# A graph layer fed by GpSimd gathers: whole-table VectorE passes move to ScalarE, and the gather ring grows from 26 to 27 quads

## What is computed

```python
h = jnp.maximum(_layernorm(x), 0.0)                      # x: 12500 nodes x 128
C = 0.5 * (jnp.cos(edge_weight * PI / CUTOFF) + 1.0)     # 212500 edges
W = (ssp(edge_attr @ mlp_w1 + mlp_b1) @ mlp_w2 + mlp_b2) * C[:, None]
xp = h @ lin1_w
agg = segment_sum(xp[src] * W, dst, num_segments=12500)  # dst is sorted
out = x + (ssp(agg @ lin2_w + lin2_b) @ lin_w + lin_b)   # ssp(v) = softplus(v) - log 2
```

## Time and profile before

| | us |
|---|---|
| median of 3 runs | 2056.18 |
| lowest and highest run | 2053.5, 2058.3 |
| the profiled execution, device time | 2054.31 |
| its span, first to last instruction | 2052.4 |
| GpSimd busy | 1539.9 |
| TensorE, VectorE, ScalarE busy | 1302.4, 1081.9, 910.0 |

### The profile page before, as it was taken

The page is one execution under the profiler, slowest core; times in us unless marked ns, Lnnn a source line. Parts: engine busy times, 40 slices in busy tenths (PEclk is TensorE's granted clock), DMA queues, the critical chain, the costliest instruction groups (busy, mean ns, idle before and its releaser), DMA issues.

```text
span 2052.4 us, 51157 instructions
## 1 busy us (share of the span) xinstructions
PE 1302.4 (63%) x12671; PEld 1108.5 (54%) x12879; DVE 1081.9 (53%) x3364; ACT 910.0 (44%) x1536; POOL 1539.9 (75%) x1629
## 2 busy tenths in 40 slices
PE   6567666766676666656666666666656556666565
PEld 5455555555555555545555555555545445555454
DVE  8766655555555555545544445545444445454444
ACT  6664444444444444444443444434443444343442
POOL 7777777777777777777777777777777777777775
PEclk9887988888888788777887877887888788787887
DMA  9632333333333333333333333333332332333321
GB/s 319 233 88 77 85 89 78 85 90 80 90 89 79 84 88 80 91 90 80 82 90 79 90 89 79 86 85 80 89 90 71 89 89 72 89 79 82 88 72 47
DMA packets 118412, 190.46 MB, mean 93 GB/s; under 512 B 34784, under 2 KB 66000, under 8 KB 117988
## 3 DMA queue, kind: packets, MB, share of 16 engines
q0 software_dynamic: 51968, 106.53, 21.0%
q1 hardware_dynamic: 63076, 79.85, 13.2%
q10 hardware_dynamic: 3072, 0.79, 0.2%
HBM read 174.24 MB, written 12.80 MB: 91 GB/s over the span
## 4 chain that ended last, share of the span: by engine, by line
POOL 37%; issue 19%; PE 11%; SPq 10%; ACT 8%; DVE 7%; ACTq 4%; DVEq 2%; DMA 1%; POOLq 0%
POOL XG L435 37%; SPq L393 7%; ACTq L508 4%; PE PA L801 3%; PE PW L787 3%; PE PX L770 3%; SPq L389 2%; ACT TB L523 2%; ACT TB L521 2%; DVE XG L684 2%; ACT TB L519 2%; DVEq L656 1%; PE PW L784 1%; ACT XG L457 1%; DVE TB L575 1%
## 5 line engine op out<-in xcount | busy, mean ns | idle before, releaser
L435 POOL DMA_INDIRECT XG<-xp_scratch,IX x1560 | 1476.0, 946 | 475.8 <-issue 469.7
L684 DVE SCALAR_TENSOR_TENSOR XG<-PW,CC,XG 128x128 f32<-128x128 f32 x1624 | 456.8, 342 | 442.4 <-DMA XG<-xp_scratch,IX 425.7
L519 ACT ACTIVATE TB<-PX 128x512 f32<-128x512 f32 x416 | 245.7, 591 | 968.8 <-PE PX L770 477.6
L787 PE MATMUL PW<-W,TB 128*128 128x128 f32 x3322 | 538.8, 315 | 106.5 <-DVE XG L684 79.4
L787 PEld LDWEIGHTS PW<-W,TB 128*128 128x128 f32 x3322 | 535.2, 230 | 18.1
L784 PE MATMUL PW<-BPB,ones 128*128 128x512 bf16 (+1 forms) x209 | 98.9, 473 | 566.3 <-DVE XG L684 548.9
L784 PEld LDWEIGHTS PW<-BPB,ones 128*128 128x128 bf16 x416 | 40.7, 98 | 744.2 <-issue 737.1
L652 DVE SCALAR_TENSOR_TENSOR TB<-PX,TB 128x512 f32<-128x512 f32 x416 | 283.9, 682 | 274.6 <-ACT TB L523 266.8
L801 PE MATMUL PA<-OH,XG 128*64 128x64 f32 x6480 | 317.7, 271 | 0.0
L523 ACT ACTIVATE TB<-TB,HALF 128x512 f32<-128x512 f32 x416 | 299.7, 720 | 13.5
L801 PEld LDWEIGHTS PA<-OH,XG 128*64 128x64 f32 x6480 | 286.8, 182 | 32.3 <-issue 21.1
(11 more groups left out here) (86 smaller groups left out, 495.2 us busy)
## 6 DMA issues: line engine op xcount, KB each, us to landing
HT<-xp_scratch SPq DMA_DIRECT2D x3092, 0.5 KB
AT<-attr_t SPq DMA_DIRECT2D x206, 200.0 KB
XG<-xp_scratch,IX POOLq DMA_INDIRECT x1560
HA<-xp_scratch ACTq DMA_DIRECT2D x1536, 0.5 KB
AG<-zero SPq DMA_DIRECT2D x1, 6400.0 KB, 22.8
xp_scratch<-XG SPq DMA_DIRECT2D x24, 256.0 KB, 2.9
XR<-x SPq DMA_DIRECT2D x24, 256.0 KB, 5.0
out<-XR SPq DMA_DIRECT2D x24, 256.0 KB, 2.6
```

What stands on the lines that cost most here:

```text
L435: e.indirect_dma_start(XG[q % XG_N][0:p, k * D:(k + 1) * D], None, xp, bass.IndirectOffsetOnAxis(ap=IX[0:p, t0 + k:t0 + k + 1], axis=0)).t ...
L519: e.activation(T[:, 0:w], PX[q % X1_N][:, 0:w], ACT.Abs).then_inc(s_ab, 1)
L684: ins = e.scalar_tensor_tensor(out=G, in0=PW[q % 2][0:p, k * D:(k + 1) * D], scalar=CC[0:p, t0 + k:t0 + k + 1], in1=G, op0=ALU.mult, op1=A ...
L787: ins = e.matmul(P[0:p, k * D:(k + 1) * D], TB[q % TB_N][:, k * TILE:k * TILE + p], W2[:, :], start=False, stop=(k == n - 1), skip_group_c ...
```

## The change

- **Ring:** XG_N goes from 26 to 27 quads.
- **Turns:** the two rounding passes leave VectorE and are two Copy activations on ScalarE (`turns`), ahead of its chunk 22. VectorE's last pass stays, and is cut into four pieces of some 416 columns. VectorE waits for `s_ck`.
- **Places:** the casts of the base and destination tables leave VectorE for ScalarE (`places`), ahead of its chunk 32. The base is also cast into a PSUM bank (`BQ`), and the subtraction that forms REL reads the base from there and not from SBUF.
- **Flags:** the test for places outside the window leaves VectorE. ScalarE takes Abs(REL - 31.5) and Relu(2|.| - 63) at step 18 (`far`), which writes VB directly. The product of flags and cutoff moves into the repair path.
- **First layer:** for quads 0 and 1 TensorE waits for the last rectifier only, not for ScalarE's last copies.

```diff
-    XG_N, TB_N, X1_N, OH_N = 26, 4, 4, 2
+    XG_N, TB_N, X1_N, OH_N = 27, 4, 4, 2
...
+        MID = sb("MID", [128, 2])
+        BQ = PF[:, 0:NQ]
...
+            def turns():
+
+                e.wait_ge(s_tb, 16)
+                e.activation(CK[:, :], CC[:, :], ACT.Copy, scale=0.05, bias=MAGIC).then_inc(s_ck, 1)
+                e.wait_ge(s_ck, 1)
+                e.activation(CK[:, :], CK[:, :], ACT.Copy, bias=-MAGIC).then_inc(s_ck, 1)
+
+            def places():
+
+                e.wait_ge(s_dx, 16 * (11 + 2 * AT_N))
+                e.activation(BF[:, :], BI[:, :], ACT.Copy).then_inc(s_di, 1)
+                e.activation(BQ, BI[:, :], ACT.Copy).then_inc(s_di, 1)
+                e.activation(REL[:, :], DI[:, :], ACT.Copy).then_inc(s_di, 1)
+
+            def far():
+
+                e.wait_ge(s_rel, 2)
+                for p, a, b in ((TILE, 0, NT - 1), (EDGES - (NT - 1) * TILE, NT - 1, NT)):
+                    e.activation(CK[0:p, a:b], REL[0:p, a:b], ACT.Abs, bias=MID[0:p, 0:1]).then_inc(s_far, 1)
+                e.wait_ge(s_far, 2)
+                for p, a, b in ((TILE, 0, NT - 1), (EDGES - (NT - 1) * TILE, NT - 1, NT)):
+                    e.activation(VB[0:p, a:b], CK[0:p, a:b], ACT.Relu, scale=2.0, bias=MID[0:p, 1:2]).then_inc(s_vb, 1)
...
-                e.wait_ge(s_cst, 1)
-                e.wait_ge(s_cw, 1)
+                e.wait_ge(s_cw, 4)
...
             for c in range(NPC + 3):
+                if c == NNC - 3:
+                    turns()
                 if c == NNC + 5:
                     cutoff()
+                if c == NNC + 7:
+                    places()
...
+                if i == FLAG_STEP:
+                    far()
...
             norms(0, NNC)
             e.wait_ge(s_tb, 16)
-            link(e.tensor_scalar(CK[:, :], CC[:, :], 0.05, MAGIC, ALU.mult, ALU.add))
-            link(e.tensor_scalar_add(CK[:, :], CK[:, :], -MAGIC))
-            e.scalar_tensor_tensor(out=CK[:, :], in0=CC[:, :], scalar=0.05, in1=CK[:, :],
-                                   op0=ALU.mult, op1=ALU.subtract).then_inc(s_cw, 1)
+            e.wait_ge(s_ck, 2)
+            for a in range(0, NT, -(-NT // 4)):
+                b = min(NT, a - (-NT // 4))
+                e.scalar_tensor_tensor(out=CK[:, a:b], in0=CC[:, a:b], scalar=0.05, in1=CK[:, a:b],
+                                       op0=ALU.mult, op1=ALU.subtract).then_inc(s_cw, 1)
...
-            e.tensor_copy(BF[:, :], BI[:, :])
-            link(e.tensor_copy(REL[:, :], DI[:, :]))
+            e.memset(VB[:, NT - 1:NT], 0.0).then_inc(s_rel, 1)
+            e.wait_ge(s_di, 3)
             nf = NT // QT
-            rel = REL[:, 0:nf * QT].rearrange("p (q t) -> p q t", t=QT)
-            link(e.tensor_tensor(rel, rel, BF[:, 0:nf].unsqueeze(2).to_broadcast([128, nf, QT]), ALU.subtract))
             if NT % QT:
                 link(e.tensor_scalar(REL[:, nf * QT:NT], REL[:, nf * QT:NT], BF[:, nf:nf + 1], None, ALU.subtract))
+            rel = REL[:, 0:nf * QT].rearrange("p (q t) -> p q t", t=QT)
+            e.tensor_tensor(rel, rel, BQ[:, 0:nf].unsqueeze(2).to_broadcast([128, nf, QT]), ALU.subtract).then_inc(s_rel, 1)
...
-                if i == FLAG_STEP:
-
-                    link(e.memset(CK[:, NT - 1:NT], 0.0))
-                    for p, a, b in ((TILE, 0, NT - 1), (tail, NT - 1, NT)):
-                        link(e.tensor_scalar(CK[0:p, a:b], REL[0:p, a:b], WIN - 0.5, None, ALU.is_gt))
-                        link(e.scalar_tensor_tensor(out=CK[0:p, a:b], in0=REL[0:p, a:b], scalar=-0.5, in1=CK[0:p, a:b],
-                                                    op0=ALU.is_lt, op1=ALU.add))
-                    link(e.tensor_copy(VB[:, :], CK[:, :]))
-                    e.tensor_tensor(CK[:, :], CK[:, :], CC[:, :], ALU.mult).then_inc(s_vb, 1)
...
-                    if q < X1_N:
+                    if q == 0:
                         e.wait_ge(s_re, NPC)
+                    elif q < X1_N:
                         e.wait_ge(s_xe, NPC)
...
-                        e.wait_ge(s_vb, 1)
+                        e.wait_ge(s_vb, 2)
```

More of the change, by code:

```diff
@@ L175, in gnn_kernel @@
         s_cst = sem("s_cst")
+        s_ck = sem("s_ck")
+        s_di = sem("s_di")
+        s_rel = sem("s_rel")
+        s_far = sem("s_far")
         s_sin = sem("s_sin")
@@ L508, in fetch @@
                     e.dma_start(HA[j % HA_N][p + i:p + i + 1, :], xp[bass.ds(v, 1), :]).then_inc(s_ra[j % HA_N], 16)
+            e.wait_ge(s_cst, 4)
             for i in range(STEPS):
@@ L544, in _ @@
             e.memset(ones[:, :], 1.0).then_inc(s_cst, 1)
+            e.memset(MID[:, 0:1], 0.5 - WIN / 2).then_inc(s_cst, 1)
+            e.memset(MID[:, 1:2], 1.0 - WIN).then_inc(s_cst, 1)
             link(e.memset(BPB[:, :, :], 0.0))
@@ L642, in plus_x @@
                 ins.then_inc(s_fo, 1)
-            tail = EDGES - (NT - 1) * TILE
             for i in range(STEPS):
@@ L748, in _ @@
             e.wait_ge(s_bq, 6)
-            e.wait_ge(s_cst, 2)
+            e.wait_ge(s_cst, 4)
             for i in range(STEPS):
@@ L831, in gnn_kernel @@
         tail = EDGES - (NT - 1) * TILE
-        flagged = nc.values_load(FL[0:1, 0:1], min_val=0, max_val=TILE)
+        flagged = nc.values_load(FL[0:1, 0:1], min_val=0, max_val=2 * TILE * NODES)
         with nc.If(flagged > 0):
+            nc.vector.memset(CK[:, NT - 1:NT], 0.0)
+            nc.all_engine_barrier()
+            for p, a, b in ((TILE, 0, NT - 1), (tail, NT - 1, NT)):
+                nc.vector.tensor_scalar(CK[0:p, a:b], REL[0:p, a:b], WIN - 0.5, None, ALU.is_gt)
+                nc.all_engine_barrier()
+                nc.vector.scalar_tensor_tensor(out=CK[0:p, a:b], in0=REL[0:p, a:b], scalar=-0.5, in1=CK[0:p, a:b],
+                                               op0=ALU.is_lt, op1=ALU.add)
+                nc.all_engine_barrier()
+            nc.vector.tensor_tensor(CK[:, :], CK[:, :], CC[:, :], ALU.mult)
+            nc.all_engine_barrier()
             nc.vector.tensor_copy(REL[:, :], DI[:, :])
@@ L882, in gnn_kernel @@
             with nc.Fori(0, NT - 1) as t:
-                found = nc.values_load(FT[0:1, bass.ds(t, 1)], min_val=0, max_val=TILE)
+                found = nc.values_load(FT[0:1, bass.ds(t, 1)], min_val=0, max_val=2 * TILE * NODES)
                 with nc.If(found > 0):
                     fix(t, TILE)
-            found = nc.values_load(FT[0:1, NT - 1:NT], min_val=0, max_val=TILE)
+            found = nc.values_load(FT[0:1, NT - 1:NT], min_val=0, max_val=2 * TILE * NODES)
             with nc.If(found > 0):
```

## The result

| | before | changed |
|---|---|---|
| median device time, 11 runs each | 2054.40 | 2049.55 |
| lowest to highest | 2053.36 to 2058.3 | 2048.78 to 2051.26 |
| span of the profiled execution | 2052.4 | 2046.3 |
| start of the last gather | 2036.72 | 2031.02 |
| from there to the end of the span | 15.7 | 15.3 |

The ratio is 0.9975, with a 95% interval of 0.9966 to 0.9984: the change is worth 4.9 us, clear of noise. The forecast was 2050.2 with a range of 2047.0 to 2054.2, and faster by more than 0.2% (4.1 us) was its likeliest case.

What follows compares the result with a forecast made beforehand. GpSimd's gather stream plus a fixed 15.7 us tail was taken to bound the kernel. Gains of 1.5 + 1.7 + 2.2 = 5.4 us from a four-execution mean of 2055.6 gave 2050.2 us, range 2047.0 to 2054.2.

Steps and rivals of the forecast that it cites:

- The bound: Whole kernel: GpSimd's gather stream plus a fixed tail sets the end; each GpSimd microsecond counts, other engines' gains nothing themselves.
- The reading of the nine gathers: GpSimd's nine gathers over 0.2 us too long: each ends a little after a VectorE whole-table pass, some 0.81 us.
- The sum: Gather losses removed in three places: 1.5 + 1.7 + 2.2 = 5.4 us gain, bounds 3.3 and 6.3.
- The turns: Gathers beside the angle's rounding passes, losing 2.36 us: gain 1.5 us, bounds 0.8 and 2.4.
- the places: Two gathers beside the table casts and the REL subtraction, losing 1.68 us: gain 1.7, bounds 0.3 and 1.7.
- the flags: Four gathers beside the far-place test at step 18: all 2.2 us of loss goes, no bound below.
- The tail: From the last gather's start to the span's end: the same 15.7 us, while the last quads are worked off.
- What ScalarE takes on: Node part and step 18: added ScalarE passes stay outside the gather stream; quad 0 starts within some 0.3 us of before.
- The ring: GpSimd's first wait for a scattered quad: 27 buffers leave about 5 us of room; 26 would stall some tenths.
- rival B: Start of the quad loop: room used up, GpSimd waits, 2.5 us lost, gain 2.9, time 2052.7; chance 0.09.
- A: Gathers beside VectorE passes: only casts and one-input passes stretch them; gain 1.9 us, time 2053.7; chance 0.06.
- C: All 1,624 gathers: their fixed pitch changes; 6 ns more is 9.7 us, time 2059.9; chance 0.05.

Runs made afterwards that it cites:

- turns_back: Changed kernel with the angle's rounding back on VectorE, in three whole passes; 2049.66 us, 0.9977 of the kernel before.
- two_sbuf: Changed kernel with the subtraction that forms REL reading the bases from SBUF instead of PSUM; 2050.14 us, 0.9982 of the kernel before.
- flags_back: Changed kernel with the test for far places back on VectorE at step 18; 2050.93 us, 0.9984 of the kernel before.
- ring26: Changed kernel with a ring of 26 quads instead of 27; 2052.82 us, 0.9994 of the kernel before.
- before_again: The kernel before, unedited, run again as a control; 2054.42 us, ratio 1.0002.
- lean_later: Changed kernel with three ScalarE instructions fewer and its two remaining casts behind the reciprocals; 3094.18 us on a slower chip, 0.9958 of the kernel before there.
- dose_two: Changed kernel with four added VectorE products of two SBUF tables (1,660 columns) at step 12; 2052.61 us, 0.9990 of the kernel before.

## Why the prediction was right, and where it was off

**The bound.** Right: every kernel on the usual chips moved its span with its last gather (1.75 and 1.7 us in turns_back, 0.62 and 0.7 in two_sbuf, 3.3 and 3.0 in flags_back, 2.4 and 3.3 in ring26), while 6.6 to 7.7 us of VectorE's own passes left no trace beyond the gathers they held.

**The reading of the nine gathers.** "Each ends a little after a whole-table pass does" holds for eight of them. Six end 0.81 or 0.82 us after a pass, and two (63.75 and 116.17) 0.11 and 0.12 us after a one-input pass that began behind them. The ninth, at 68.40, starts 1.1 us after L603 is over: it stands beside VectorE's short ops L609 and L611, and its 0.2 us of loss is still there in the changed kernel.

**The sum.** The turns were forecast with 1.5 us and gave 2.36 - 0.77 = 1.6; the places 1.7 and 1.7; the flags 2.2 and 2.2. Together 5.4, and 5.5 measured, with the last gather at 2031.02 where 2031.3 was forecast. The second part of the stream began at 84.35 (84.7 forecast). The flags had no range at all, one value read from one execution; the same passes cost 2.55 us in before_again and 3.2 in flags_back. That the changed profile set against the first one gives 2.2 again is no test of it, since both numbers are the loss of that first profile.

**The tail** was forecast as "the same 15.7 us" and was 15.3. It is not fixed to that degree: the kernel before has 15.7 in one execution and 14.6 in the other. **The time outside the span**, which the forecast took as fixed at 1.9 us by adding the gain to device times, rose by 1.4. The 5.7 us of the stream and the 0.4 of the tail less that 1.4 make 4.7, within 0.2 of the 4.9 us measured.

**Luck.** The forecast started from a mean of four runs, 2055.6, that was 1.2 us above the median of eleven. From that median it would have been 2049.0, half a microsecond below the 2049.55 measured instead of 0.65 above it. So the gain was right in its mechanism, but that 5.4 lies so near 4.9 and 2050.2 so near 2049.55 is in part luck: the start was too high by 1.2, the stream and the tail gave 0.7 more, and 1.4 us went where the prediction had no term.

**What ScalarE takes on.** The step "quad 0 starts within some 0.3 us of before" failed. Timelines of ScalarE and of TensorE in the changed kernel:

```profile
123.62 1.22 ACT L463 ACTIVATE XG<-PW,RS 128x128 f32<-128x128 f32 x4
124.61 0.71 ACT L552 ACTIVATE TB<-PX 128x512 f32<-128x512 f32 x1
```

```profile
136.13 1.15 PE L831 MATMUL PA<-OH,XG 128*64 128x64 f32 x32
```

The first Abs does follow the last copy directly, but at 124.61, not near 122.7, and quads 0 and 1 are scattered from 136.13 instead of 134.05. Two single executions can't show the size of this, for the kernel before scattered them from 137.39 in before_again. What does repeat is the stretch behind the casts. I had counted ScalarE's 2.4 us of casts, and not the longer wait that they give TensorE and what its clock does after it. In the changed kernel TensorE waited 3.83 us for VectorE in this stretch:

```profile
102.36 1.11 PE L760 MATMUL PX<-EYE,TB 128*128 128x128 f32 x4 [3.83 <-DVE TB L612]
...
104.97 1.06 PE L760 MATMUL PX<-EYE,TB 128*128 128x128 f32 x4
```

In the kernel before the same wait was 1.16 us, and the four transposes behind it took 0.66 us. The windows of 99 to 112 us (length, busy us, granted clock, DMA share, GB/s), the changed kernel first, then the kernel before, read

```profile
99.00:112.00 13.00, 8.24 (x48) 0.74 0.61 169
```

```profile
99.00:112.00 13.00, 9.06 (x72) 1.00 0.66 179
```

Before, the whole stretch was at the upper level, 2.4 GHz; now about half of it was at 1.2 GHz (an estimate from the mean of 0.74), and the four transposes took 1.11 us instead of 0.66.

The other profiles of the usual chips say the same. In all eight of the changed family TensorE waited 3.3 to 4.1 us at this place and the four transposes took 1.11 or 1.12 us; in the two of the kernel before it waited 1.16 and 1.62 us and they took 0.66. From these transposes to ScalarE's last copy are 20.7 and 20.5 us in the kernel before, and 22.1 to 23.0 in the eight others. So the missing term is 1.3 to 2.5 us. That the clock is its cause is argued from these rows and was not tried apart; lean_later was to do that, and ran on a chip where it can't be read.

**The ring.** The room was forecast at 5 us. GpSimd came to quad 27 at 139.34 and quad 0 had been scattered by 136.7, so it was 2.6; and quad 0 itself moves by 3.3 us between the two executions of the kernel before, which no room worked out from one profile allows for. The stall with 26 buffers was put at "some tenths" and is 2.8 us in ring26. That was the nearest the change came to rival B: with the 27th buffer no profile of the usual chips shows GpSimd waiting for a scatter beyond its 0.3 us, and without it the ratio is no longer clear of no change.

**The rivals.** A (only one-input passes hold gathers) is refuted by two_sbuf and dose_two. C (the pitch) by the window of GpSimd that answers to the earlier trace rows:

```profile
1000.00:2032.00 1032.00, 780.06 (x827) 0.80 0.32 83
```

1032.00 / 827 = 1.248 us a gather, as before.

## What to carry to other kernels

Where an engine does nothing but issue DMAs back to back, look at its durations one by one, not at its waits: nine stretched instructions among 1,624 were nearly the whole of this gain, and eight of them pointed to the pass of another engine that ended just before they did. A pass beside such a stream can be moved, cut into pieces, or given an input in PSUM. All three shortened the losses, and the last left VectorE's pass as it was, at the price of one cast of 0.6 us on ScalarE. When a stream gets earlier, check at once what it runs into, here its own ring, and compare spans as well as device times, since they need not move together.

## What the runs showed of the hardware that I had not expected

- The time outside the span has two levels, 1.7 to 1.8 and 2.9 to 3.2 us, which follow the program and not the chip. In the changed family it follows ScalarE's number of instructions, in the kernel before nine more don't raise it. What sets it stays open.
- The kernel before needs 2054 us on the other chips and 3106.53 us on one, where SyncE takes 25.50 us for 32 row fetches in one place, and up to 36 in others, instead of 16.15. Why that chip is slower wasn't looked into.
- A gather beside consecutive passes with two SBUF inputs is held once, near its start, for the rest of the pass: 1.49, 1.62, 1.62 and 1.62 us in dose_two.
- Passes with one SBUF input (L602, L619, L729 of flags_back) also held gathers that were already under way, which then ended 0.11 to 0.12 us after the pass. A one-input reduction of 1.87 us on one partition held none.
